# Fused cross-attention and gated feed-forward on one core: two moves in the step that is written out by hand before the loop

## The reference, cut to what matters

```python
x = x + xattn(layernorm(x), ctx_768, Wq, Wk, Wv, Wout, bout)
x = x + ffn(layernorm(x), W_r, W_k, W_v, mu_r, mu_k)

# xattn, 8 heads of 128; the keys of both batches are used together (154 of them)
qh, kh, vh = split_heads(x @ Wq), split_heads(ctx @ Wk), split_heads(ctx @ Wv)
sim = einsum('hid,hjd->hij', qh, kh) * 128**-0.5
sim = (sim - mean(sim)) * 1.5 + mean(sim)
attn = softmax(sim, axis=-1)
return merge_heads(einsum('hij,hjd->hid', attn, vh)) @ Wout + bout

# ffn
x_prev = x shifted down by one row in its sequence (zeros first)
xr = mu_r * x + (1 - mu_r) * x_prev
xk = mu_k * x + (1 - mu_k) * x_prev
r = sigmoid(xr @ W_r.T)
return r * (square(relu(xk @ W_k.T)) @ W_v.T)
```

## Time and profile before

| what | value |
|---|---|
| median of 3 runs | 754.74 us |
| the profiled execution's own time | 754.75 us |
| its span in the profile | 752.9 us |
| PE busy | 745.0 us (99%) |
| DVE busy | 510.5 us (68%) |
| ACT busy | 425.1 us (56%) |
| POOL busy | 121.8 us (16%) |
| the chain that ended last, by engine | PE 85%, DVE 6%, ACT 5%, issue 2%, POOL 1%, DMA 1% |

### The profile page before, as it was taken

The page is one execution under the profiler, slowest core; times in us unless marked ns, Lnnn a source line. Parts: engine busy times, 40 slices in busy tenths (PEclk is TensorE's granted clock), DMA queues, the critical chain, the costliest instruction groups (busy, mean ns, idle before and its releaser), DMA issues.

```text
span 752.9 us, 13609 instructions
## 1 busy us (share of the span) xinstructions
PE 745.0 (99%) x3996; PEld 650.7 (86%) x3996; DVE 510.5 (68%) x1071; ACT 425.1 (56%) x1199; POOL 121.8 (16%) x279
## 2 busy tenths in 40 slices
PE   8999999989999999999999999999999999999998
PEld 8976888888888889888888989898898988888887
DVE  2658686677776766677766666777766677776662
ACT  3677647464755656464655746466475646555432
POOL 1110011212102021211112121210202121020211
PEclk9999999999999999999999999999999999999999
DMA  9933434543445354543544454344435444343301
GB/s 304 364 107 116 153 117 148 165 143 123 149 133 161 108 160 142 164 126 114 160 124 131 146 164 143 121 141 132 149 112 174 132 142 142 117 147 104 109 30 43
DMA packets 84216, 106.54 MB, mean 142 GB/s; under 512 B 9791, under 2 KB 61017, under 8 KB 84187
## 3 DMA queue, kind: packets, MB, share of 16 engines
q1 hardware_dynamic: 84187, 106.19, 44.7%
HBM read 58.70 MB, written 47.45 MB: 141 GB/s over the span
## 4 chain that ended last, share of the span: by engine, by line
PE 85%; DVE 6%; ACT 5%; issue 2%; POOL 1%; DMA 1%; SPq 0%; POOLq 0%; DVEq 0%; ACTq 0%
PE ffn L479 11%; PE ffn L481 11%; PE ffn L480 11%; PE scores L480 8%; PE scores L481 8%; PE scores L479 8%; PE attended L481 7%; PE attended L480 7%; PE attended L479 7%; ACT probs L765 2%; PE scores L659 1%; ACT probs L774 1%; PE attended L517 1%; PE attended L516 1%; DVE xk L1084 1%
## 5 line engine op out<-in xcount | busy, mean ns | idle before, releaser
L480 PE MATMUL scores<-A_lo,xT_hi 128*128 128x462 f32 (+1 forms) x384 | 134.5, 350 | 0.0
L479 PE MATMUL scores<-A_hi,xT_hi 128*128 128x462 f32 (+1 forms) x384 | 134.2, 349 | 0.0
L481 PE MATMUL scores<-A_hi,xT_lo 128*128 128x462 f32 (+1 forms) x384 | 134.1, 349 | 0.0
L765 ACT ACTIVATE probs<-scores,neg_max 128x154 f32<-128x154 f32 x256 | 96.4, 389 | 40.3 <-DVE neg_max L1028 39.9
L481 PE MATMUL attended<-B_hi,pT_lo 128*128 128x512 f32 x288 | 112.4, 390 | 0.0
L480 PE MATMUL attended<-B_lo,pT_hi 128*128 128x512 f32 x288 | 112.3, 390 | 0.0
L479 PE MATMUL attended<-B_hi,pT_hi 128*128 128x512 f32 x288 | 112.0, 389 | 0.0
L1028 DVE TENSOR_REDUCE neg_max<-scores 128x3 f32<-128x462 f32 (+1 forms) x96 | 55.0, 582 | 78.7 <-PE scores L481 78.7
L1303 POOL TENSOR_SCALAR var<-stats 128x1 f32<-128x1 f32 x64 | 12.3, 192 | 472.3 <-DVE stats L975 471.2
L479 PEld LDWEIGHTS scores<-A_hi,xT_hi 128*128 128x128 f32 x384 | 72.4, 189 | 7.3 <-issue 0.8
L480 PEld LDWEIGHTS scores<-A_lo,xT_hi 128*128 128x128 f32 x384 | 72.3, 188 | 5.8
(11 more groups left out here) (177 smaller groups left out, 1567.5 us busy)
## 6 DMA issues: line engine op xcount, KB each, us to landing
prob_rows<-probs SPq DMA_DIRECT2D x32, 704.0 KB, 3.4
probs_handed<-prob_rows SPq DMA_DIRECT2D x128, 176.0 KB, 3.3
x_rows<-normed SPq DMA_DIRECT2D x61, 256.0 KB, 2.1
handed<-x_rows SPq DMA_DIRECT2D x244, 64.0 KB, 1.9
x_in<-in_x SPq DMA_DIRECT2D x32, 256.0 KB, 3.5
out<-x SPq DMA_DIRECT2D x31, 256.0 KB, 2.2
wq<-in_L_xattn_Wq SPq DMA_DIRECT2D x4, 512.0 KB, 8.8
wout<-in_L_xattn_Wout SPq DMA_DIRECT2D x1, 2048.0 KB, 15.9
```

The source lines that it names most:

```text
L479: te.matmul(psum, left[0], right[0], start=first, stop=False)
L480: te.matmul(psum, left[0], right[1], start=False, stop=False)
L481: return te.matmul(psum, left[1], right[0], start=False, stop=last)
L765: last = nc.scalar.activation(probs[:, q, cols], S[b][:, (h - h0) * J:(h - h0 + 1) * J], ACT.Exp, bias=neg_max[:, h:h + 1], accum_out=row_ ...
```

## The change

On DVE, `x_lo(5)` and `add_x(2, 0, 2)` (the addition with the statistics of x2 of tile 2, the third tile) stand ahead of the maxima of tile 4 (the fifth). On ACT, `mixed_high("r", 1, 1)` stands ahead of all exponentials of tile 4, and `x2_norm(2, 2)` between the second and the third bank's exponentials. Nothing is added or taken out, and PE's, POOL's and SP's lists are as they were.

```diff
@@ ACT @@
             mixed_high("k", 1, 1)
+            mixed_high("r", 1, 1)
             exponentials(4, 0)
-            mixed_high("r", 1, 1)
             exponentials(4, 1)
+            x2_norm(2, 2)
             exponentials(4, 2)
             normalise_early(4)
             pack_hi(4)
             open_gate(0, 0, 2)
-            x2_norm(2, 2)
             for i in range(3):
                 probs_hi(3, i)
             squares(0, 0)
@@ DVE @@
             mixed_low("k", 1, 1)
+            x_lo(5)
+            add_x(2, 0, 2)
             for b in range(3):
                 maxima(4, b)
-            x_lo(5)
             mixed_low("r", 1, 1)
             inverse_early(4)
             normalise_late(4)
             pack_lo(4)
-            add_x(2, 0, 2)
             probs_turn(3)
             for i in range(3):
                 probs_lo(3, i)
```

## The result

The changed kernel takes 756.37 us (median of 17 runs, 754.09 to 758.39), the kernel before 754.31 us (17 runs, 752.26 to 755.63). The ratio is 1.0028 with a 95% interval of 1.0020 to 1.0036: slower by about 2 us. The median lies just inside the range forecast for 8 in 10, 753.3 to 756.5, and above the forecast's own 754.6 to 755.6. What was held most likely, no difference beyond 1.5 us, did not come.

A forecast was written before the change was run, and what follows sets the result against it. PE was taken as the bound, with a gap at key_columns(1). Terms of +0.2 (split of pT) and +0.1 (late load) lengthened it by 0.3 us, giving 755.0 us; own range 754.6 to 755.6, 8 in 10 753.3 to 756.5.

The forecast's parts named there:

- What bounds the kernel: PE, busy 745.0 of 752.9 us; its 1.9 us gap at key_columns(1) plus 1.7 us of lost clock behind it.
- Parts 1 to 3: DVE maxima 2.22 us later; ACT copy takes 0.51 off the path; norm between exponentials adds 0.72; normalise_early(4) 2.43 later.
- The term forecast at +0.2: Start of pT_hi of tile 3 on ACT: 118.7 instead of 118.50, behind probs_turn(3); bounds 0.0 to 0.4 us.
- Part 4: SP: load of tile 6 goes about 2.3 us later, behind store_probs(4); priced +0.1 us, ends 0 and 0.5.
- the load's term: Landing of tile 6's load, needed by x_statistics(6): free up to 121.9, 0.4 us at 122.3; +0.1 taken.
- So no new gap: PE at tile 3's attention: first low part in time by 0.6 us; other low parts and score banks needed later.
- Rival 3: Load of tile 6 late beyond the ends; each microsecond behind 121.9 costs one; 122.9 gives 755.9 us; chance 0.10.
- Rivals 1 and 2: Behind the gap: 1, clock does not fall, 753.3 us, chance 0.11; 2, half clock twice as long, 756.7, chance 0.12.

The follow-up runs named there:

- xr_pool: The kernel before with xr_hi of tile 1 ahead of tile 4's exponentials on ACT and x_root(t + 3) ahead of output(q - 1, 1) on POOL: 751.84 us, 0.9963.
- sp_early: The changed kernel with load_x(6) and store_x2(2) ahead of store_probs(4) in SP's list: 755.09 us, 1.0007 of the kernel before.
- load_early: The changed kernel with only load_x(6) moved ahead of store_probs(4) in SP's list: 754.18 us, 0.9993 of the kernel before.
- late_load: The kernel before with only load_x(6) moved back behind store_x2(2) in SP's list: 755.59 us, 1.0009 of the kernel before.
- store_early: The changed kernel with store_x2(2) ahead of store_probs(4) in SP's list, load_x(6) left late: 755.53 us, 1.0015 of the kernel before.
- xr_only: The kernel before with only the ACT copy xr_hi of tile 1 moved ahead of tile 4's exponentials: 752.67 us, 0.9973.
- dve_only: The changed kernel's DVE order with the ACT order of the kernel before: 755.83 us, 1.0010 of the kernel before.
- the filled kernels: Unused matmuls on PE at the end of step t = 3: 8 in the kernel before, 753.21 us; 12 in the changed kernel, 754.38 us.
- after_fill: The changed kernel with 17 unused matmuls on PE at the end of step t = 3: 754.99 us.
- after_fill12: The changed kernel with 12 unused matmuls on PE at the end of step t = 3: 754.38 us.

## Why the prediction was right and where it was wrong

**What bounds the kernel: right.** From xr_pool to after, the medians in the table follow the time at which PE goes on, but for two neighbouring pairs (sp_early and load_early, late_load and store_early), and 17 matmuls in front of the gap make before and after equal.

**Parts 1 to 3 and their sum: right.** From the anchor the maxima started at 2.82 (2.82 worked out), `normalise_early(4)` at 7.16 (7.21), pT_hi at 11.50 (11.55), released by the transposition and no longer by POOL. The term forecast at +0.2 measured +0.15. The norm between exponentials took 0.70.

**Part 4: this is the step that failed.** It priced the late probabilities by the statistics and the exponentials of tile 5 alone, and left out the reader that comes behind both, `x_turn(6)`.

On SP: "The stores and reads of x2 of tile 2 behind it move by less than the several microseconds that their readers leave." That looked at the readers of x2 alone. In SP's order `store_x(6)` and `hand_x(6)` come behind them, and their reader, `x_turn(6)`, had next to no slack: xr_only, which speeds everything ahead of it by 0.54, gets 0.24 and a wait. The turned rows came 1.67 late from the anchor in the changed kernel. That is the whole of PE's 1.66.

On the norm of tile 6: the load's term, "I take +0.1, with 0 and 0.5 as ends", was not mis-sized for the path it looked at. The landing was foreseen, 3.9 us after the issue at 117.77. From the anchor the statistics started at 14.26, before the limit of 14.7 worked out for a delay without cost, and the exponentials of tile 5 came 0.33 late against the +0.3 of all terms. But the norm must also be through for `store_x(6)`, and it ended 1.16 late. Of this 0.55 is POOL's shift of tile 6, which took 0.82 us instead of the 0.27 of the earlier trace rows that Part 4 carried over.

"So no new gap" failed by the same step, at the scores of tile 6, whose turned rows were late. The terms said +0.3 in all; PE was 1.66 later.

**Rival 3** named the load, but as a landing beyond the ends, priced through the statistics only. The landing stayed within the ends. load_early and late_load confirm the place; the way from there to the loss was missing.

**How far the number was luck.** The sum missed 1.4 us of PE's time in the profiled pair. The median of 756.37 lies in the range because the range had been widened by the rivals on the clock, not because its cause was foreseen.

**Rivals 1 and 2, the clock: both happened.** The clock did not fall in 2 of 17 runs (754.1 and 754.4 us, forecast 753.3), and it fell for twice as long in 4 of 17 (757.7 to 758.4, forecast 756.7), the profiled execution among them. Both forecasts are low, by 0.8 to 1.1 and by 1.0 to 1.7 us, near the 1.4 us that Part 4 missed. The rival tied the second fall to the length of the gap; the length does not decide alone. The profiled executions of dve_only and store_early, with gaps of 2.8 us, had a clock of 1.00 throughout, and so had load_early's behind 2.20, while that of before fell behind 1.93. What the Trainium skill says of the clock's monitor (TensorE: Matmul & The Clock Gate, What's actually happening), that it runs freely beside the kernel, fits this: the same instructions gave three levels of time. The means of the groups are 754.25, 756.20 and 758.04 us. The steps of 1.95 and 1.84 us are near one fall of the clock, which the rows before put at 1.7.

The changed kernel's runs at a clock of 1.000 are 754.1 and 754.4 us. Of 89 runs of before in the three sets beside the experiments, 13 had 0.999 or 1.000; they are 752.2 to 753.2, with a mean of 752.6. The means are 1.7 us apart, the filled kernels 1.2: that is the change itself, without the clock. The rows gave 1.66 and, in the filled pair, 0.95.

## What to carry to other kernels

When a step is moved, list all that its DMA queue still has behind it, down to the next step, and write each one's slack beside it; here a load and a read for another tile paid. A small load that used to leave in a quiet moment can cost its place when it lands behind a large store: issue it as soon as its buffer is free, whatever the program's order was. And one gap of the engine that bounds the kernel can cost twice, by itself and by the clock behind it, so compare runs by their granted clock before comparing kernels.

## What the runs showed that I had not expected

POOL's `shift` of tile 6, 0.27 us in the kernel before, took 0.81 to 0.85 us in after, dve_only, after_fill and after_fill12. In after it is the only one of its line over 0.4 us between 60 and 750 us, and DVE's subtraction of the squares (123.33 to 124.62) ran beside it. In store_early and late_load, where it comes behind that subtraction, it took 0.27; but there the two small operations ahead of it fell beside the subtraction (123.08 to 124.37 in late_load) and took longer instead, 0.64 and 0.88 us against 0.19 and 0.55:

```profile
123.18 0.64 POOL L1308 TENSOR_SCALAR var<-stats 128x1 f32<-128x1 f32 x1 [5.24 <-DVE stats L980]
123.91 0.88 POOL L1310 TENSOR_TENSOR rstd<-var,minus_half 128x1 f32<-128x1 f32 x1
```

In these six kernels each small operation of POOL that starts during DVE's subtraction is 0.3 to 0.6 us longer than in before, where none does, and it stands on the path to the norm. That the one disturbs the other was not tested by itself.

The store of x2, 256 KB, took 2.0 us to land in before and 4.1 right behind 960 KB of others in the same list; the load of tile 6, also 256 KB, took 2.5 in load_early with nothing right in front and 3.9 (after) and 4.8 (store_early) when issued 0.4 us behind the 704 KB store.

A float32 matmul of 128 columns from the identity is two instructions on PE, 0.24 us at the full clock.
